# A graph network on one core: one gathered tile of 64 per turn fetched row by row by SyncE

## The reference, cut to what matters

```python
def gat_conv(x, ei, W, a_src, a_dst, b, heads, out_ch):
    h = (x @ W).reshape(n, heads, out_ch)
    alpha_src = jnp.sum(h * a_src, axis=-1)
    alpha_dst = jnp.sum(h * a_dst, axis=-1)
    e = jax.nn.leaky_relu(alpha_src[src] + alpha_dst[dst], 0.2)
    m = jax.ops.segment_max(e, dst, num_segments=n)
    ex = jnp.exp(e - m[dst])
    s = jax.ops.segment_sum(ex, dst, num_segments=n)
    alpha = ex / (s[dst] + 1e-16)
    out = jax.ops.segment_sum(alpha[:, :, None] * h[src], dst, num_segments=n)
    return out.reshape(n, heads * out_ch) + b
```

## Time and profile before

| | us |
|---|---|
| median of 2 runs | 18844.35 |
| lowest, highest | 18838.42, 18850.27 |
| profiled execution: span, first to last instruction | 15220.1 |
| median less that span | 3624.2 |

### The profile page before, as it was taken

The page is one execution under the profiler, slowest core; times in us unless marked ns, Lnnn a source line. Parts: engine busy times, 40 slices in busy tenths (PEclk is TensorE's granted clock), DMA queues, the critical chain, the costliest instruction groups (busy, mean ns, idle before and its releaser), DMA issues. The chain is left out here.

```text
span 15220.1 us, 212898 instructions
## 1 busy us (share of the span) xinstructions
PE 7563.9 (50%) x51680; PEld 6275.1 (41%) x51680; DVE 6961.0 (46%) x24545; ACT 6200.7 (41%) x13834; POOL 11256.0 (74%) x11885
## 2 busy tenths in 40 slices
PE   5555552556564963444432444442344442766666
PEld 3444441555554862333332333332333332433334
DVE  6555554777775973333345333335222224433333
ACT  4777761677774842222221222221122222333333
POOL 5777776777776777777767777777777776777776
PEclk7777775887886965666655666665555555777777
DMA  5444442222222943444442444443333333333333
GB/s 186 162 162 162 163 152 73 96 93 92 91 93 84 347 157 119 147 148 148 147 127 87 147 148 148 148 147 68 82 85 85 85 85 71 108 119 119 119 119 93
DMA packets 939375, 1906.89 MB, mean 125 GB/s; under 512 B 438162, under 2 KB 517037, under 8 KB 898165
## 3 DMA queue, kind: packets, MB, share of 16 engines
q1 hardware_dynamic: 490085, 854.45, 17.0%
q0 software_dynamic: 356624, 523.18, 15.0%
q10 hardware_dynamic: 92240, 525.31, 8.7%
HBM read 1041.86 MB, written 889.14 MB: 127 GB/s over the span
## 5 line engine op out<-in xcount | busy, mean ns | idle before, releaser
L113 POOL DMA_INDIRECT eg_got<-gat_table,edge_rows x4983 | 4706.1, 944 | 1533.4 <-issue 1502.9
L113 POOL DMA_INDIRECT e_got<-table,edge_rows x3322 | 3142.3, 946 | 1044.2 <-issue 998.6
L1624 PE MATMUL eg_ps_sum<-eg_got,eg_equal 128*128 128x136 f32 (+1 forms) x9984 | 2219.0, 402 | 0.0
L1624 PEld LDWEIGHTS eg_ps_sum<-eg_got,eg_equal 128*128 128x128 f32 x9984 | 2114.7, 310 | 30.2 <-issue 1.3
L1639 ACT ACTIVATE eg_outs<-eg_ps_sum 128x544 f32<-128x544 f32 (+1 forms) x1248 | 683.9, 548 | 3397.3 <-PE eg_ps_sum L1624 3395.7
L118 POOL DMA_INDIRECT sorted_rows<-sort_rows,sort_dest x1661 | 1612.1, 971 | 506.3 <-issue 506.3
L1688 DVE COPY eg_own<-eg_got 128x128 f32<-128x128 f32 (+1 forms) x312 | 68.6, 220 | 3420.2 <-DMA eg_got<-gat_table,edge_rows 3420.2
L1669 PE MATMUL eg_up<-ident,eg_own 128*128 128x128 f32 (+1 forms) x312 | 137.4, 440 | 2567.9 <-DVE eg_own L1688 2567.9
L1669 PEld LDWEIGHTS eg_up<-ident,eg_own 128*128 128x128 f32 (+1 forms) x312 | 47.3, 152 | 2650.5 <-issue 2537.5
L1718 ACT ACTIVATE eg_equal<-eg_equal_b 128x512 f32<-128x512 bf16 x1248 | 782.4, 627 | 482.5 <-issue 482.5
L686 PE MATMUL e_ps_sum<-e_got,e_equal 128*128 128x64 f32 x3328 | 567.5, 329 | 686.7 <-DMA e_got<-table,edge_rows 686.5
(11 more groups left out here) (510 smaller groups left out, 20397.0 us busy)
## 6 DMA issues: line engine op xcount, KB each, us to landing
gat_out<-eg_outs ACTq DMA_DIRECT2D x208, 1152.0 KB
eg_equal_b<-equal_d SPq DMA_DIRECT2D x312, 512.0 KB
out<-e_outs ACTq DMA_DIRECT2D x104, 1024.0 KB
values<-e_zeros_b SPq DMA_DIRECT2D x104, 768.0 KB
values_q<-e_zeros_b SPq DMA_DIRECT2D x104, 768.0 KB
sort_value<-values_q SPq DMA_DIRECT2D x104, 768.0 KB
e_value<-values SPq DMA_DIRECT2D x104, 768.0 KB
eg_got<-gat_table,edge_rows POOLq DMA_INDIRECT x4983
```

Source lines behind the costliest of these rows:

```text
L113: return e.indirect_dma_start(out, None, table, bass.IndirectOffsetOnAxis(ap=index, axis=0), **kw)
L1624: last_i = e.matmul(ps_sum[q % 2][:, i, 0:FG], equal[q % 4][:, i, :], got[k][:, t, :], start=True, stop=True)
```

## The change

In the three attention passes POOL gathers 63 tiles instead of 64 in each of the 25 looped turns. The last tile of the fourth group comes another way. SP loads the 128 node numbers of that tile (one row of a small table, `fetch_ids`) into SBUF, moves them into registers eight at a time, and issues one DMA of one table row for each, 32 in front of each k, into a tile `fetch_rows`. DVE copies that tile in two halves (64 partitions each) into `got[3][:, 15, :]`, ahead of its waits for groups 2 and 3. The table `fetch_ids` is made once, at the start of `first_pass`, by a DMA of 26 x 128 single numbers. The last turn is gathered as before.

SP's other loads are put in another order. Matrices of group k-1 are brought behind the row fetches of k (before: of group k at the end of k), the patch of the turn before is stored at k = 1 (before: the turn's own at its end), and `bring_ends` comes at k = 1 (before: at the head of the turn).

```diff
+class RowFetch:
+    PARTS = len(G4)
+    AT_ONCE = 8
...
+    def bring_ids(self, e, it):
+        e.dma_start(self.ids[:, :], self.kn.fetch_ids[bass.ds(it, 1), :]).then_inc(self.ids_in.sem, 16)
+
+    def sync(self, e, it, part):
+        n = P // self.PARTS
+        if part == 0:
+            e.wait_ge(self.ids_in.sem, self.ids_in.at(it, 1))
+        if part % 2 == 0:
+            e.wait_ge(self.moved.sem, self.moved.at(it, part // 2 - 1))
+            e.sem_inc(self.asked, 1)
+        for p0 in range(part * n, (part + 1) * n, self.AT_ONCE):
+            loads, ids = self.kn.nc.values_load_multi_w_load_instructions(
+                self.ids[0:1, p0:p0 + self.AT_ONCE], engines=[mybir.EngineType.SP], min_val=0, max_val=NP - 1,
+                skip_runtime_bounds_check_because="edge ends are node numbers, as in the gathers")
+            for p, node in enumerate(ids, p0):
+                e.dma_start(self.rows[p:p + 1, :], self.table[bass.ds(node, 1), :]).then_inc(self.fetched[part].sem, 16)
+        if part == self.PARTS - 1:
+            self.bring_ids(e, it + 1)
...
+    def move(self, e, it, half, to):
+        for part in (2 * half, 2 * half + 1):
+            e.wait_ge(self.fetched[part].sem, self.fetched[part].at(it, 1))
+        some = slice(half * P // 2, (half + 1) * P // 2)
+        e.tensor_copy(to[some, :], self.rows[some, :]).then_inc(self.moved.sem, 1)
...
+            e.dma_start(self.fetch_ids[0:TURNS, :], source[len(G4) - 1::len(G4), :, GT - 1, 1]).then_inc(fetch_ids_made, 16)
...
+        own_tiles = [GT, GT, GT, GT - 1]
+        fetch = RowFetch(self, ph, table, FG)
...
+            fetch.bring_ids(e, 0)
             with e.Fori(0, TURNS - 1) as it:
-                bring_ends(it)
                 for k in G4:
-                    g = bass.ds(it * len(G4) + (len(G4) + k), 1)
+                    fetch.sync(e, it, k)
+                    if k == 1:
+                        store_patch(it - 1, 0)
+                    before = (k - 1) % n4
+                    e.wait_ge(equaled.sem, equaled.at(it, k * QUADS))
+                    bring_equal(bass.ds(it * n4 + (before if k == 0 else n4 + before), 1), before)
+                    g = bass.ds(it * n4 + (n4 + k), 1)
                     e.wait_ge(value_up.sem, value_up.at(it, k + 1))
                     bring_value(g, k)
+                    if k == 1:
+                        bring_ends(it)
                     e.wait_ge(repeated.sem, repeated.at(it, k + 1))
                     e.wait_ge(gathered[k].sem, gathered[k].at(it, 1))
                     e.dma_start(rows[k][:, :, :], source[g, :, :, :].rearrange("g p t c -> (g p) t c")).then_inc(rows_in[k].sem, 16)
-                    e.wait_ge(equaled.sem, equaled.at(it, (k + 1) * QUADS))
-                    bring_equal(g, k)
-                store_patch(it, 0)
...
             with e.Fori(0, TURNS - 1) as it:
                 for k in G4:
-                    group(it, k, GT)
+                    group(it, k, own_tiles[k])
...
+                if mid in (2, 3) and not last_turn(it):
+                    e.wait_ge(summed.sem, summed.at(it, QUADS - 1))
+                    fetch.move(e, it, mid - 2, got[n4 - 1][:, GT - 1, :])
+                    if mid == 3:
+                        e.wait_ge(fetch.moved.sem, fetch.moved.at(it, 2))
```

More of the change, by code:

```diff
@@ L139, in row_numbers, with arrived, __init__, end @@
     e.wait_ge(ve, c(1))
-def arrived(gathered, it, k):
+def arrived(gathered, tiles, it, k):
     buf, turn = k % len(G4), k // len(G4)
-    missing = GT - REAL[buf] if isinstance(it, int) and it + turn == TURNS - 1 else 0
+    missing = tiles[buf] - REAL[buf] if isinstance(it, int) and it + turn == TURNS - 1 else 0
     return gathered[buf].at(it, 1 + turn) - 16 * missing
+class RowFetch:
+    PARTS = len(G4)
+    AT_ONCE = 8
+    def __init__(self, kn, ph, table, width):
+        self.kn, self.table = kn, table
+        self.ids, self.rows = ph.sb("fetch_ids", [1, P], I32), ph.sb("fetch_rows", [P, width])
+        self.ids_in = Tally(ph, "fetch_ids_in", 1, 16)
+        self.fetched = [Tally(ph, f"fetched{k}", 1, 16 * P // self.PARTS) for k in range(self.PARTS)]
+        self.moved = Tally(ph, "fetch_moved", 2, ahead=2)
+        self.asked = ph.sem("fetch_asked")
+    def bring_ids(self, e, it):
[15 more added lines that the diff above has]
+            self.bring_ids(e, it + 1)
+    def end(self, e):
+        e.wait_ge(self.ids_in.sem, 16 * TURNS)
+    def move(self, e, it, half, to):
[3 more added lines that the diff above has]
+        e.tensor_copy(to[some, :], self.rows[some, :]).then_inc(self.moved.sem, 1)
 def broadcast_row(row, n):
@@ L209, in constants @@
         self.links_d = self.dram("links_d", (T, P), BF16)
+        self.fetch_ids = self.dram("fetch_ids", (TURNS, P), I32)
         self.attr_copied = self.nc.alloc_semaphore("attr_copied")
@@ L464, in sync @@
             e.wait_ge(cleared, 3 * NG * 16)
+            e.wait_ge(fetch_ids_made, 16)
             e.wait_ge(again, 4 * 16)
@@ L680, in pe_sums @@
             k, tiles = at(q)
-            e.wait_ge(gathered[buf(k)].sem, arrived(gathered, it, k))
+            e.wait_ge(gathered[buf(k)].sem, arrived(gathered, [GT] * len(G4), it, k))
             e.wait_ge(equaled.sem, equaled.at(it, q + 1))
@@ L1450, in gat_pass @@
         rows_in = [Tally(ph, f"rows_in{k}", 1, 16) for k in G4]
-        gathered = [Tally(ph, f"gathered{k}", 1, 16 * GT) for k in G4]
+        own_tiles = [GT, GT, GT, GT - 1]
+        fetch = RowFetch(self, ph, table, FG)
+        gathered = [Tally(ph, f"gathered{k}", 1, 16 * own_tiles[k]) for k in G4]
         stored = [Tally(ph, f"stored{k}", 2, 48, ahead=16) for k in B2]
@@ L1553, in sync @@
                 e.sem_inc(rows_in[k].sem, 16)
-            e.sem_inc(patched.sem, patched.ahead)
             for k in G4:
                 bring_value(bass.ds(k, 1), k)
+            for k in range(n4 - 1):
                 bring_equal(bass.ds(k, 1), k)
@@ L1600, in sync @@
             e.wait_ge(again, 4 * 16)
+            fetch.end(e)
         def gpsimd(e):
@@ L1891, in vector @@
         def vector(e):
+            e.sem_inc(fetch.moved.sem, fetch.moved.ahead)
             for made in (message, masked, spread, added):
```

17 lines of the change are left out of this document (10 added, 7 removed).

## The result

The changed kernel takes 22,070.98 us (median of 2 runs, 22,063.09 to 22,078.87) against 18,844.35: a ratio of 1.171, 95% interval 1.169 to 1.173. That is 17% slower, far above the forecast of 18,760 and above the range's end of 19,750.

The account below looks back on a forecast made before the run. POOL's back-to-back gathers were taken to bound the attention passes. Three passes falling from 2074 to 2043 us, plus 10 us for a later start, gave -84 us: 18844 - 84 = 18,760 us, range 18,720 to 19,750.

Parts of the forecast that it names:

- 25 S + 38: Attention pass in us if SP sets the pace: 25 turns of SP's time S, forecast 80.0, plus finishing group 3.
- The 0.43 us a row: SP's one-row DMAs, issue to issue with register operation and MOVE: 128 x 0.43 = 55.0 us a turn.
- the second rival: SP's one-row issues hold one another up: 68.5 us for 128, S = 93.5, 19,760 us; chance 0.11.
- The loop's end: SP's larger loop body stands still 2.9 us at each turn's end, 2.6 more than before.
- SP and POOL are all but equal: Turn times in the attention passes: SP 80.0 us, POOL 78.6, with POOL still setting the pace by 5 us a pass.
- signs of being wrong: POOL's gathers wait for PE's sums, DVE's copy waits for SP, loads well above 0.5 us or issues well above 0.25.
- 16 x 0.74 = 11.8: SP's 16 register loads a turn, assuming eight numbers cost what one does, 0.74 us: 11.8 us.
- the first rival: Each number of SP's register loads costs: 1.56 us a load, S = 93.2, 19,740 us; chance 0.27.
- the long waits between are left out: they are slack: SP's long waits within a turn were counted as nothing, as room in which the new work can lie.
- the DMAs that stay: SP's 16 remaining DMAs a turn, summed with other small work to 10.6 us.
- I take 10: Start of the first pass: the node-number table delays it 7 to 26 us; 10 us taken, once.
- the median lies 3624 us above the span, and nothing of the change is in that part: The timed median exceeds the profile's span of 15220.1 us; that excess was taken as untouched by the change.

Follow-up runs that it names:

- e3_no_loads: Changed kernel with each fetched row's number computed from the turn's number, so no register loads; quick set, 15,205.27 us, -18 against the kernel before.
- e6_one_per_load: Changed kernel with one number per register load instead of eight, 128 loads a turn; slow set, 25,775.22 us, +6772 against the kernel before.
- e13_after: The changed kernel, unaltered, run in a quick set: 16,053.6 us against 15,228.01 for the kernel before.
- e7_sixteen_per_load: Changed kernel with sixteen numbers per register load instead of eight, 8 loads a turn; slow set, 21,987.4 us, +2984 against the kernel before.
- e14_straight: Changed kernel with 384 semaphore increments a turn in place of loads and fetches, 64th tile not fetched; quick set, 15,176.16 us beside 15,228.01 before.
- e4_fixed_rows: Changed kernel fetching 128 constant rows, without register loads, register operations or MOVEs; quick set, 15,170.78 us, -53 against the kernel before.
- e2_reorder_only: Changed kernel with SP's new load order kept, but no row fetches and POOL gathering all 64 tiles; quick set, 15,251.41 us, +28 against the kernel before.

## Why the prediction was wrong

**Right.** What bounds the kernel before: POOL's gathers, back to back, and what 63 of them are worth: 2043 us a pass, 2044 to 2048 measured wherever SP was out of the way in a quick set. The form of the sum: a pass is the larger of POOL's time and 25 S + 38, within 12 us in the quick set and some 50 in the slow one. The 0.43 us a row: 57.0 instead of 55.0 us, so the second rival (issues holding one another up) falls; a one-row load takes 228 ns in the median. The loop's end, 2.9 against 3.4 in the quick set. That a taken branch to code outside the loaded pages waits for a fetch is what the Trainium skill ("Runtime: NRT & Kernel Launch", Instruction fetch mechanics) states; the trace agrees, with the 3.4 us behind the branch and 763 packets of kind "instruction" against 369 before. The reordering, free. And "SP and POOL are all but equal" was the true weak point: every miss from there on counts 25-fold in a pass. Three of its signs of being wrong came true: POOL waits for PE's sums, DVE's copy of the fetched rows waits for SP, 24 us a turn where "a few us longer" than 12 was said, and a load takes well above 0.5 us.

**Wrong in a quick set, +826 us where -84 was forecast.** The terms of S:
- "16 x 0.74 = 11.8": a load of eight takes 782 ns in the median and not 466, and 0.95 us in the mean of the first pass (single ones take 1.4 us and more), with its gap 1.0 us, 16.0 in all, 4.2 more. That further numbers cost is the mechanism of the first rival, at a smaller size; `e3_no_loads` shows that without the loads nothing is lost.
- "the long waits between are left out: they are slack": before the change SP waited for ACT with time to spare; in the changed kernel SP has no spare time, and 5.2 us a turn of that wait stay, behind work that SP's own transfers start. The forecast priced it at nothing. It is the largest missed term. That the chain from fetch to conversion is its cause is read from two timelines, and no run removed it.
- the rows +2.0, the DMAs that stay +1.4, the loop's end +0.5.

Together 13.4 us, S = 93.4, and S may be at most 81.4 before the gain is lost. Its size is by chance that of the rivals (93.2, 93.5): the first has a part in it, 4.2 of 13.4 us, the second none. The table of node numbers: "I take 10" of 7 to 26, measured 32.

**Wrong in the timed runs, +3227 us.** The step that failed is "the median lies 3624 us above the span, and nothing of the change is in that part". The kernel before in a quick set has a time 2 us off its span; the 3624 us are no fixed amount at either end but lie in the passes: 427, 1138 and 693 us in three that the change doesn't touch. Where the kernel was timed it takes 24% longer than where it was profiled, and durations of the one were added up and applied to the other. There SP's turn is 136.1 us and not 93.4, all of the difference in the 384 short instructions of the fetch, while the other engines' turn is 93.5.

Shown by the runs: this loss comes with the instructions that SP executes, transfers or not (16 transfers cost nothing, 128 bare ones +562 us, 384 increments +1218, the whole fetch +3227), and in time only once the stops have used up SP's waits; it isn't the length of the code, and it isn't the transfers as such. Open: what stops SP for multiples of some 0.7 us, and what makes a set slow, since the chip by its number doesn't decide it. Recording the profile may have a part in it; no run went without.

No version that computes the same beat the kernel before. With fixed rows it is 0.35% faster in a quick set and 3% slower in a slow one, with increments in place of the fetch 0.3 to 0.4% faster and 6 to 9% slower, and all of these leave the right rows out.

## What to carry to other kernels

Before a profile's durations are added up, lay its span beside the timed median: where they differ by thousands of us, as here, the profile and the times may not be of the same conditions, and the gap may be spread over every term of the sum. Work moved to a queue that "only waits" ends up behind its waits as well as in them: count the queue's turn with each wait that its own work starts. And trading one 1.25 us gather for 128 transfers of 0.4 us each pays only while the second queue has more idle time than that in every turn.

## What the runs showed of the hardware

- A register load from SBUF takes 494, 782 and 1171 ns (medians; `e6_one_per_load`, `e13_after`, `e7_sixteen_per_load`) for 1, 8 and 16 numbers.
- One-row loads whose row comes from a register are issued every 0.41 us on SP in the median, 228 ns of it the issue, and every 0.45 in the mean (`e13_after`).
- At the end of a loop's turn SP stands still for 3.3 us in the median with some 450 to 470 instructions in the body, and for 0.2 or less with 65 to 198 (`e13_after`, `e14_straight`; before, `e4_fixed_rows`).
- The same program takes 15,220 to 15,250 us in some sets of runs and 18,840 to 19,000 in others; the busy times of DVE, ACT and POOL are alike, and what differs is time between instructions, with single register operations of 0.7 and 1.4 us that take 29 to 43 ns in a quick set.
- 384 semaphore increments of 17 ns a turn on a queue that otherwise waits cost nothing in a quick set and 1218 us in a slow one.
- A DMA of 26 x 128 single numbers in front of the first loads delays the first gather by 32 to 35 us (201.3 us before; 233.4 in `e2_reorder_only`, 236.5 in `e4_fixed_rows`).
